# One block instead of two for routing and the experts of a mixture-of-experts layer

## The reference, cut to what matters

```python
logits = jnp.einsum('th,eh->te', x, gate_w)
scores = jax.nn.softmax(logits, axis=-1)
topk_w, topk_idx = jax.lax.top_k(scores, K)          # K = 2 of E = 16
combine = jnp.sum(jax.nn.one_hot(topk_idx, E) * topk_w[..., None], axis=1)
# each expert e: y_e = (silu(x @ w_gate[e]) * (x @ w_up[e])) @ w_down[e], inner size 176
```

## Time and profile before

| what | us |
|---|---|
| median of 3 runs (1219.4 to 1220.78) | 1220.33 |
| the profiled execution's own time | 1228.29 |
| its span | 1226.0 |
| route block, by its instructions | 736.81 to 803.89 |
| experts block, by its instructions | 804.39 to 941.6 |
| of it, first down product to the last output's copy | 824.19 to 939.40 |

### The profile page before, as it was taken

One profiled execution on the slowest core, in us unless ns is written; L12 is line 12 of the kernel. 1 busy time (PEld: TensorE's weight loads), 2 busy tenths in 40 slices (PEclk: granted clock), 3 DMA queues, 4 the chain that ended last, 5 costly groups with the idle time before them and its releaser, 6 DMA issues. The chain is left out here.

```text
span 1226.0 us, 19866 instructions
## 1 busy us (share of the span) xinstructions
PE 1142.5 (93%) x7044; PEld 998.7 (81%) x7044; DVE 764.6 (62%) x1612; ACT 510.6 (42%) x963; POOL 238.8 (19%) x274
## 2 busy tenths in 40 slices
PE   5999999999999999999999976849999769999997
PEld 4988989889898898988989865737776559878897
DVE  4765656657567475575656686924445686686655
ACT  5576343443334344343343556112221256553322
POOL 1112110101101010010100100023332562322211
PEclk9999999999999999999999988869999868999999
DMA  4001001001000000000000008053343233100001
GB/s 146 10 1 35 10 1 35 9 0 43 0 22 21 0 34 9 0 34 9 0 1 1 1 1 293 1 137 105 106 107 101 57 98 108 36 1 1 18 18 35
DMA packets 29306, 50.33 MB, mean 41 GB/s; under 512 B 5216, under 2 KB 19520, under 8 KB 27968
## 3 DMA queue, kind: packets, MB, share of 16 engines
q1 hardware_dynamic: 25216, 38.81, 9.5%
q0 software_dynamic: 3840, 10.49, 3.3%
q10 hardware_dynamic: 192, 0.26, 0.1%
HBM read 36.70 MB, written 10.49 MB: 38 GB/s over the span
## 5 line engine op out<-in xcount | busy, mean ns | idle before, releaser
L619 POOL TENSOR_TENSOR linear_out_squares<-linear_out_squares,lin_sq 128x512 f32<-128x512 f32 x64 | 91.2, 1426 | 599.0 <-ACT lin_sq L520 596.1
L41 PE MATMUL lin_bank<-keep_xT_hi,lin_w_hi 128*128 128x512 f32 x384 | 155.6, 405 | 2.6 <-DVE keep_xT_lo L230 2.6
L575 DVE TENSOR_TENSOR lin_st<-lin_bank,lin_mask 128x512 f32<-128x512 f32 x64 | 44.3, 692 | 175.2 <-PE lin_bank L430 175.2
L42 PE MATMUL lin_bank<-keep_xT_lo,lin_w_hi 128*128 128x512 f32 x384 | 152.8, 398 | 0.0
L43 PE MATMUL lin_bank<-keep_xT_hi,lin_w_lo 128*128 128x512 f32 x384 | 152.5, 397 | 0.0
L516 ACT ACTIVATE lin_o<-lin_bank 128x512 f32<-128x512 f32 x64 | 38.3, 599 | 189.9 <-PE lin_bank L461 189.9
L457 PE MATMUL lin_bank<-lin_st,lin_v 128*128 128x128 f32 x512 | 94.0, 275 | 0.0
L41 PEld LDWEIGHTS lin_bank<-keep_xT_hi,lin_w_hi 128*128 128x128 f32 x384 | 73.0, 190 | 18.0 <-issue 3.0
L43 PEld LDWEIGHTS lin_bank<-keep_xT_hi,lin_w_lo 128*128 128x128 f32 x384 | 72.7, 189 | 17.8
L461 PE MATMUL lin_bank<-lin_qd,lin_state 128*128 128x128 f32 x448 | 87.2, 276 | 0.0
L42 PEld LDWEIGHTS lin_bank<-keep_xT_lo,lin_w_hi 128*128 128x128 f32 x384 | 72.9, 190 | 14.7
(11 more groups left out here) (378 smaller groups left out, 2835.2 us busy)
## 6 DMA issues: line engine op xcount, KB each, us to landing
lin_raw<-in_wp SPq DMA_DIRECT2D x8, 1024.0 KB, 4.8
sorted_y<-linear_out_acc SPq DMA_DIRECT2D x48, 128.0 KB
experts_up_expert_up<-in_wgu SPq DMA_DIRECT2D x16, 352.0 KB, 7.3
experts_down<-in_wdn SPq DMA_DIRECT2D x16, 176.0 KB
keep_x<-in_x SPq DMA_DIRECT2D x4, 512.0 KB, 7.5
lin_raw_out<-in_wop SPq DMA_DIRECT2D x8, 256.0 KB, 2.7
tokens_x<-linear_out_acc SPq DMA_DIRECT2D x4, 512.0 KB, 10.4
linear_out_acc<-in_ffn_up SPq DMA_DIRECT2D x2, 1024.0 KB, 5.7
```

Of the source, the lines that this page charges most:

```text
L41: nc.tensor.matmul(out, lh, rh, start=first, stop=False, skip_group_check=skip)
L42: nc.tensor.matmul(out, lh, rl, start=False, stop=False, skip_group_check=skip)
L575: dve.tensor_tensor(C4(st[:, a, :]), C4(bank[2 + a][:]), mask[:, a:a + 1, :].broadcast_to([P, TPS, P]), ALU.mult).then_inc(st_sb, 1)
L619: pool.tensor_tensor(part, part, sq[:, a, :], ALU.add).then_inc(squares_sb, 1)
```

## The change

Routing and the experts become one block. In detail:

- The down weights have no buffer of their own now: one row of 8192 elements per partition holds `acc` (4096), `squares` (2048) and a new buffer `more` (2048), and the same bytes, on 88 partitions, are the weights of the 16 experts. Experts 0 to 7 lie in `acc`, 8 to 11 in `squares` (the row one-hots of b = 0 and b = 1), 12 to 15 in `more` (token one-hots of b = 0 and b = 1, the router's gate weights and `upto`). 
- The 16 loads become six: two of 4 experts once the tokens are stored and turned, two of 2 experts once the matmuls of b = 0 are done, two of 2 experts once those of b = 1 are done.
- `pe_tokens` is called once for each b: b = 0 before the last two `pe_down`, b = 1 after them.
- On DVE, `dve_tiles` is split into `dve_passed` (the comparison) and the rest; the order is now comparison, `dve_tokens`, the rest. `slot_token` and `expert_of` get semaphores.
- POOL, after its constants, waits for the stores and for `slot_token`, and gathers. PE waits for `expert_of` and goes on with its loop. The loop itself and those of ACT, DVE and SP are as before, with other places for the buffers (rows gathered in the dead `z_y`, the rest in the shared expert's `silu`, `h` and `loaded`).
- `k2` of the tail lies in `more`; three semaphores (`k_zero`, `v_zero`, `v_one`) move to the outermost scope.

```diff
+FOLLOWING = {"linear_out": (("acc", "squares", "more"), SEGS * KT * SEG + TOK + 2048)}
...
+        keep.more = c.sb("more", [P, 2048])
+        keep.expert_down = c.row[0:IH, :].rearrange("p (e n f) -> p e n f", e=NE, n=2)
...
-    def pe_tokens(self, pe):
-
-        pe.wait_ge(self.row_hot_ready, 2)
-        pe.wait_ge(self.token_hot_ready, 2)
-        for b in range(2):
-            for t in range(TT):
+    def pe_tokens(self, pe, b):
+
+        pe.wait_ge(self.row_hot_ready, b + 1)
+        pe.wait_ge(self.token_hot_ready, b + 1)
+        for t in range(TT):
...
     def dve_tokens(self, dve, chain):
-        dve.wait_ge(self.tokens_mm, 1)
+        dve.wait_ge(self.tokens_mm, 2)
...
-        chain.link(dve.tensor_copy(self.keep.slot_token[:], self.token_f[:]))
+        dve.tensor_copy(self.keep.slot_token[:], self.token_f[:]).then_inc(self.slot_token_ready, 1)
...
+    def sp_load(self, sp, w_down, first, end):
+        sp.dma_start(self.down_w[:, first:end], w_down[first:end].rearrange("e i n f -> i e n f")).then_inc(self.down_in, DMA)
...
                 sp.wait_ge(stored, SEGS * DMA)
+                sp.wait_ge(norms.turned, KT * SEGS)
+                work.sp_load(sp, expert_down, 0, 4)
+                work.sp_load(sp, expert_down, 4, 8)
+                sp.wait_ge(router.tokens_mm, 1)
+                work.sp_load(sp, expert_down, 8, 10)
+                work.sp_load(sp, expert_down, 12, 14)
+                sp.wait_ge(router.tokens_mm, 2)
+                work.sp_load(sp, expert_down, 10, 12)
+                work.sp_load(sp, expert_down, 14, 16)
+                work.sp_store(sp)
...
                 router.pool_constants(pool)
+                pool.wait_ge(stored, SEGS * DMA)
+                pool.wait_ge(router.slot_token_ready, 1)
+                work.pool_gather(pool)
...
                 router.dve_token_one_hot(dve, chain, 1)
+                router.dve_passed(dve, chain)
+                router.dve_tokens(dve, chain)
                 router.dve_tiles(dve, chain)
-                router.dve_tokens(dve, chain)
+                work.dve(dve)
...
                 net.act_output(act, SHARED_EARLY - 1)
+                work.act(act)
...
+                router.pe_tokens(pe, 0)
                 net.pe_down(pe, *STEPS[-2])
                 net.pe_down(pe, *STEPS[-1])
-                router.pe_tokens(pe)
...
+                router.pe_tokens(pe, 1)
+                pe.wait_ge(router.tiles_ready, 1)
+                work.pe(pe)
```

More of the change, by code:

```diff
@@ L9 @@
+import math
 import numpy as np
@@ L56, in __init__ @@
         self.nc, self.name, self.stack, self.sems = nc, name, ExitStack(), []
+        self.row, self.row_names, self.row_used = None, (), 0
     def __enter__(self):
         self.stack.__enter__()
+        if self.name in FOLLOWING:
+            names, size = FOLLOWING[self.name]
+            self.row, self.row_names, self.row_used = self.sb("row", [P, size]), names, 0
         return self
@@ L72, in sb @@
     def sb(self, name, shape, dt=F32):
+        if name in self.row_names:
+            first, self.row_used = self.row_used, self.row_used + math.prod(shape[1:])
+            part = self.row[:, first:self.row_used]
+            if len(shape) == 4:
+                part = part.rearrange("p (a b c) -> p a b c", a=shape[1], b=shape[2])
+            return part
         return self.stack.enter_context(self.nc.sbuf_tensor(f"{self.name}_{name}", shape, dt))
@@ L1198, in __init__ @@
         self.passed = self.tile_hot.rearrange("p a b -> p (a b)").rearrange("p (s e) -> p s e", e=NE)[0:1]
-        self.token_hot = [c.sb(f"token_hot{b}", [P, TT, 2, SLOT_TILES], BF16) for b in range(2)]
+        self.token_hot = [more[:, b * (HOT + 2 * ROW):b * (HOT + 2 * ROW) + HOT].bitcast(BF16).rearrange("p (t a s) -> p t a s", t=TT, a=2) for b in range(2)]
         self.row_no, self.slot_tile_no, self.token_tile_no, self.part_no = (
@@ L1202, in __init__ @@
         self.token_f = c.sb("token_f", [P, SLOT_TILES])
-        self.rows_ready, self.row_hot_ready, self.token_hot_ready, self.tokens_mm = (
-            c.sem(n) for n in ("rows", "row_hot", "token_hot", "tokens_mm"))
+        self.rows_ready, self.row_hot_ready, self.token_hot_ready, self.tokens_mm, self.slot_token_ready, self.tiles_ready = (
+            c.sem(n) for n in ("rows", "row_hot", "token_hot", "tokens_mm", "slot_token", "tiles"))
         self.zeroed, self.gate_in, self.gate_hi, self.gate_lo, self.made, self.logits_mm, self.logits_sb, self.logits_T_mm = (
@@ L1399, in close_attention_and_route, with experts @@
 def close_attention_and_route(nc, keep, y, output, norms, w_up, w_down, gate_w, tokens_x, expert_up):
+    keep.route = y, output, norms, w_up, w_down, gate_w, expert_up
+def experts(nc, keep, expert_down, tokens_x, sorted_y):
+    y, output, norms, w_up, w_down, gate_w, expert_up = keep.route
     with Scope(nc, "route") as c:
```

270 lines of the change are left out of this document (137 added, 133 removed).

## The result

| | before | changed |
|---|---|---|
| median of 5 runs, us | 1220.33 (1219.4 to 1221.03) | 1213.19 (1212.54 to 1214.87) |
| profiled execution, us | 1228.29 | 1213.64 |
| its span, us | 1226.0 | 1211.7 |
| route block's first instruction | 736.81 | 737.01 |
| first down product | 824.19 | 816.07 |

The ratio is 0.9948, with a 95% interval of 0.9935 to 0.9961: about 6.3 us faster, at least 4.8 and at most 7.9. I forecast 1212.3 us (1209.8 to 1216.8). The profiled executions differ by 14.3 us in their spans, the medians by 7.1; the tail's start moved by 8.14.

What follows compares the result with a forecast made beforehand. The experts' loop was taken as PE-bound, leaving 800 to 824 us to win. 1.36 + 1.21 + 3.33 + 2.35 - 0.2 = 8.05 us off the median of 1220.3 gave 1212.3 us, range 1209.8 to 1216.8.

Steps and rivals of the forecast that it cites:

- Step 1: At the route's end, 16 of 32 token matmuls move ahead of the last two pe_down: slot_token 1.36 us earlier.
- Step 2: Block boundary between slot_token and first gather removed: lag 0.27 us instead of 1.48, a gain of 1.21 us.
- The rule of the Trainium skill: At the first gather, DVE's instructions could lock GpSimd out: at most 0.4 us later, the sum 7.65 instead of 8.05.
- Step 3: Second gather's rows, with few loads left beside them, land in 4.0 us instead of 7.33: a gain of 3.33 us.
- rival (a): At the first gathers, the last loads delay the second by 7.33 us: 3.33 us lost, 1215.6 us; chance 0.12.
- Step 4: First down product no longer waits for the down weights, issued earlier: 2.35 us go.
- Step 5: expert_of, now after slot_token, ready at about 804.1 us while PE waits for rows until 807: costs nothing.
- Step 6: Clearing the route block's semaphores moves to the joint block's end: 0 to 0.98 us given back, 0.2 taken.
- rival (b): In the first tiles, PE's clock returns at 819.4 us all the same: 2.7 us lost, 1215.0 us; chance 0.08.
- rival (d): Joint block starts earlier, but the blocks behind lose it again: about 1219.5 us; chance 0.07.
- Rival (c): Experts' loop slower with its buffers moved, 0.25 us exposed per tile, 12.0 us on top: 1224.3 us; chance 0.05.

Runs made afterwards that it cites:

- unsplit: The changed kernel with all 32 token matmuls together behind the last two down products again; 1212.44 us, ratio 0.9948 to the kernel before.
- before_split: The kernel before with only the split token matmuls and DVE's order comparison, slot_token, rest of the tiles; ratio 1.0001 to the kernel before.
- pool_awake: The changed kernel with a small memset on POOL just before it waits for slot_token; ratio 0.9950 to the kernel before.
- combined: The changed kernel with a small POOL memset before its wait for slot_token, and the last two loads behind the first turned tile; ratio 0.9946 to the kernel before.
- two_blocks: The changed kernel cut in two blocks again behind the router, the gathers waiting for the block's end; 1213.53 us, ratio 0.9950 to the kernel before.
- tiles_first: The changed kernel with dve_tiles wholly before dve_tokens, as before the change; ratio 0.9947 to the kernel before.
- last_after_rows: The changed kernel with the last two loads issued only after PE has turned the first two tiles; 1212.19 us, ratio 0.9949 to the kernel before.
- loads_only: The change's buffers and early loads alone, with two blocks, matmuls together and DVE's order as before; ratio 0.9944 to the kernel before.
- all_late: The changed kernel with all six down-weight loads issued only after the matmuls of b = 1; 1222.93 us, ratio 1.0032 to the kernel before.

## Why the prediction was right, step by step

**What bounds the kernel.** Right: the loop kept its length (117.43 us instead of 117.45 from the first down product to the tail), and what was won lay between 800 and 824 us.

**Step 1, the token matmuls.** 1.29 us from the matmuls' start to the end of the cast (3.51 before, 2.22 after), forecast 1.36. The first 16 took 0.85 us, near the 0.7 that I took for a full clock, and the two `pe_down` behind them cost the path nothing. But what I credited to the move is worth nothing that can be measured in time (unsplit, before_split), and separate waits without the move made `slot_token` earlier still (unsplit).

**Step 2, the boundary.** The step that failed in its size: a lag of 0.90 us instead of 0.27, outside my upper bound of 0.6. The row that I took it from was a gather 0.28 us behind PE's transposes, of a POOL that had stood idle for 1.86 us. The engine here had stood idle for 64 us, and pool_awake and combined, with 0.30 us after 2.45 us of idleness, show that this is the difference. The removal of the boundary gave 0.58 us instead of 1.21, and two_blocks shows that putting it back costs nothing that can be measured.

**The rule of the Trainium skill** (SBUF — State Buffer, Who interferes with whom, its practical consequences) on DVE locking GpSimd out: here the first gather started 0.90 us after the cast and lasted 1.21 us, both beside three DVE instructions and beside none (tiles_first). No row of this case shows POOL held up by DVE, and the sum without it was the one to take. If there is a price, DVE may be the one that pays it: in pool_awake and combined, where DVE began the cast of `expert_of` 0.78 us after the gather's start instead of 0.24, that cast took 0.41 us instead of 0.18. No run shows that the gather was the reason, and nothing waited for the cast.

**Step 3, the landing.** The second tile was turned 3.37 us after its gather's start instead of 4.0, right behind the first, whose rows took 4.40 us. From gather to up product -3.57 us against my -3.33. The last two loads still cost 0.89 us there (last_after_rows), which bears out rival (a)'s mechanism at a quarter of its price. My rate for the loads, 211 GB/s, was one of loads and gathers together; the first eight experts' loads, alone on the engines, came at 164 and lasted from 766 to nearly 776 us, some 10 us where I had said 7. Nothing hung on it.

**Step 4, the down weights.** The 2.35 us went, and 0.66 us more between the first two products (7.14 to 6.48 us), because the clock came back 3.3 us after the first up product instead of 4.7. Steps 3 and 4 are the early loads, and they carry the change: they alone bring the tail forward by 6.61 us (loads_only), and without them (all_late) the others end in a loss.

**Step 5, `expert_of`.** Ready at 804.25 us, forecast 804.1, with PE waiting for rows until 808.23. Nothing, as forecast.

**Step 6, given back.** Nothing: 0.02 us the other way in the first pair, 0.00 in the second. I had set 0.2.

**The clock.** It returned at about 812.9 us, forecast near 813.5. (The price of rival (b) was misworked: from 813.5 to 819.4 us are 5.9 us and not 5.4, so that it would have cost 2.9 us instead of 2.7.) Rival (b), that the clock comes back no earlier, was wrong for the change as a whole (819.4 before) and fits what the smaller parts bring. I had priced the sum as if each term moved the first down product; among the kernels with early loads an up product that started up to 3 us sooner didn't move it in proportion.

**The sum and the median.** 8.34 us in one pair of profiles and 7.35 in the other, forecast 8.05; the ratio says 4.8 to 7.9 us, so that the time lies in the range that I gave, while 8.05 us itself is just outside the interval. That the sum came so near the first pair is in part luck: steps 1 and 2 were 0.20 and 0.63 us too large, steps 3 and 4 were 0.24 and 0.66 too small, step 6 took off 0.22 that were not lost. And 2.57 of the 8.05 us were credited to steps 1 and 2, and loads_only is as fast without them but for the separate waits. Nor does the upper end of the forecast's own range, 1214.5 us, follow from the bounds named for it: at the lower bounds of steps 2, 3 and 6 (0.88, 0 and 0.98 given back) 3.61 us are left, or 1216.7. Whether a few tenths to a microsecond are lost behind the tail's start, as in rival (d), or only two executions' scatter lies between, stays open: with a stall of 6 to 10 us behind it that comes and goes, the profiles can't tell. Rival (c), a slower loop, had nothing in it.

## What to carry to other kernels

Look first for a load that could have been issued long before and lacks only a place for its data: dead buffers gave all of the gain that could be measured here, 6 to 7 us, while an elaborate joint block gave none. Ask of each step that brings an engine sooner to the same missing input or the same slow clock whether anything of it reaches the end; here nothing measurable did, and in one profile (all_late) a longer wait let the clock drop and cost more. Take a lag from a row in which the engine had been idle as long as it will be in the new place.

## What the runs showed of the hardware that I had not expected

With an idle wait of 3.50 us PE lost its clock and 2.6 us more in the loop behind it (all_late, one profile); with one of 2.35 us at the same place it kept it. POOL started a gather 0.90 us after its semaphore when idle for 64 us, and 0.30 us after it when idle for 2.45.

The down loads are slow for their size. The DMA view of the changed kernel from 769 to 774 us, when only they run, beside 740 to 764 us, when SP loads the up weights and then stores the tokens:

```profile
DMA packets 404, 0.82 MB, mean 164 GB/s; under 512 B 11, under 2 KB 11, under 8 KB 403
...
q1 hardware_dynamic: 403, 0.80, 72.6%
```

```profile
DMA packets 5058, 8.86 MB, mean 369 GB/s; under 512 B 399, under 2 KB 2785, under 8 KB 5056
...
q1 hardware_dynamic: 5056, 8.84, 99.6%
```

164 GB/s on 72.6% of the engines' time, beside 369 GB/s on 99.6%. The Trainium skill, DMA: Bandwidth & Descriptors, Why a DMA increments its semaphore by 16 and not by 1, says of the number of engines that a transfer is spread over that it is the largest up to 16 that divides the slowest dimension of both sides; for the 88 partitions here that is 11 of 16, or 69%. The trace agrees: a down load leaves 11 packets under 512 B (the 11 above are those of the first load), and the 72.6% are near 69%, though a little above. The up loads lie on 128 partitions and fill the engines. That explains only a part of the difference in rate (the packets differ too, 2 KB for the down weights, 2.8 and 1 KB in the other stretch), and a layout of the down weights on all 16 wasn't tried.
